# Where the side work of an attention loop stands: extra steps of VectorE, TensorE and ScalarE moved to the slots with long matmul bursts, and two small products moved from VectorE to ScalarE

## The reference

```python
x = x + tanh(g_xattn) * xattn(layernorm(x), ctx, mask, mask, Wq, bq, Wk, bk, Wv, bv)
x = x + tanh(g_ffn)   * ffn(layernorm(x), W2, scale, scale1)

# xattn: 16 heads of 32 channels
q, k, v = Wq @ t + bq, Wk @ s + bk, Wv @ s + bv
dot  = (q^T k) / sqrt(32); dot = mask * dot - (1 - mask) * 1e6
out  = (softmax(dot) * mask) @ v^T

# ffn: both inputs rounded to FP8, then one matmul
q1, q2 = (layernorm(x) * scale).astype(FP8), (W2 * scale1).astype(FP8)
return (q1 / scale) @ (q2 / scale1)
```

## Time and profile before

| | us |
|---|---|
| median of three runs | 2848.67 |
| the profiled execution's own time | 2844.43 |
| its span, first to last instruction | 2842.6 |
| TensorE busy / VectorE busy | 2643.0 / 2155.0 |
| GpSimd busy / ScalarE busy | 1726.9 / 1456.4 |

### The profile page before, as it was taken

One profiled execution on the slowest core, in us unless ns is written; L12 is line 12 of the kernel. 1 busy time (PEld: TensorE's weight loads), 2 busy tenths in 40 slices (PEclk: granted clock), 3 DMA queues, 4 the chain that ended last, 5 costly groups with the idle time before them and its releaser, 6 DMA issues. The chain is left out here.

```text
span 2842.6 us, 41049 instructions
## 1 busy us (share of the span) xinstructions
PE 2643.0 (93%) x13364; PEld 1373.5 (48%) x13425; DVE 2155.0 (76%) x3314; ACT 1456.4 (51%) x2574; POOL 1726.9 (61%) x1265
## 2 busy tenths in 40 slices
PE   5999999959999999999999999999999999999995
PEld 4888888834444444444444444444444444444441
DVE  5666666656787878778888888888878888788873
ACT  3333333315555555555555555555555555555553
POOL 2333333416676767667767667677667667667774
PEclk8999999959999999999999999999999999999998
DMA  6666666454333333333333333334434443333301
GB/s 213 244 233 222 237 246 233 178 118 84 70 78 80 81 82 77 77 77 77 77 77 78 77 77 81 85 80 87 86 79 84 86 87 82 77 77 77 78 28 38
DMA packets 208249, 306.12 MB, mean 108 GB/s; under 512 B 41240, under 2 KB 108888, under 8 KB 208064
## 3 DMA queue, kind: packets, MB, share of 16 engines
q1 hardware_dynamic: 195920, 265.80, 38.8%
q10 hardware_dynamic: 12144, 38.02, 3.8%
HBM read 200.09 MB, written 102.11 MB: 106 GB/s over the span
## 5 line engine op out<-in xcount | busy, mean ns | idle before, releaser
L965 POOL TENSOR_TENSOR pair_sum<-probs 128x512 f32<-128x512 f32 x1024 | 1359.2, 1360 | 618.5 <-ACT probs L802 618.5
L866 DVE TENSOR_REDUCE part_max<-x_bank 128x1 f32<-128x512 f32 x2048 | 1308.5, 681 | 401.3 <-PE x_bank L709 394.3
L802 ACT ACTIVATE probs<-s_bank 128x512 f32<-128x512 f32 x2048 | 1129.2, 600 | 877.1 <-PE s_bank L696 859.9
L709 PE MATMUL x_bank<-k_st,q_st 98*128 98x512 f32 x2048 | 889.5, 438 | 114.4 <-DVE part_max L866 75.1
L696 PE MATMUL s_bank<-q_st,k_st 100*128 100x512 f32 x2048 | 899.0, 441 | 10.3 <-ACT probs L802 5.2
L696 PEld LDWEIGHTS s_bank<-q_st,k_st 100*128 100x128 f32 x2048 | 390.2, 191 | 490.2 <-issue 240.8
L709 PEld LDWEIGHTS x_bank<-k_st,q_st 98*128 98x128 f32 x2048 | 394.2, 193 | 387.1 <-DVE part_max L866 275.4
L722 PE MATMUL o_bank<-probs,v_t 128*32 128x512 f32 x4096 | 552.2, 612 | 0.0
L733 PE MATMUL d_bank<-pair_sum,ones 128*32 128x512 f32 x2048 | 267.8, 595 | 0.9 <-POOL pair_sum L965 0.9
L321 POOL TENSOR_TENSOR stage_lo<-stage,stage_hi 128x512 fp32r<-128x512 f32 x128 | 187.4, 1487 | 120.3 <-ACT stage_hi L391 119.6
L391 ACT ACTIVATE stage_hi<-stage 128x512 fp32r<-128x512 f32 x128 | 79.9, 633 | 190.7 <-DVE stage L475 142.1
(11 more groups left out here) (98 smaller groups left out, 2277.5 us busy)
## 6 DMA issues: line engine op xcount, KB each, us to landing
k_st<-k_scr SPq DMA_DIRECT2D x96, 512.0 KB
q_st<-q_scr SPq DMA_DIRECT2D x192, 256.0 KB
c_raw<-in_ctx_dram ACTq DMA_DIRECT2D x32, 512.0 KB, 7.1
x_raw<-in_x_dram ACTq DMA_DIRECT2D x32, 512.0 KB, 6.1
k_scr<-stage_hi SPq DMA_DIRECT2D x64, 256.0 KB, 2.4
k_scr<-stage_lo SPq DMA_DIRECT2D x64, 256.0 KB, 2.6
v_scr<-stage SPq DMA_DIRECT2D x64, 256.0 KB, 2.7
q_scr<-stage_hi SPq DMA_DIRECT2D x64, 256.0 KB, 2.1
```

Of the source, the lines that this page charges most:

```text
L709: nc.tensor.matmul(x_bank_of("tile", k)[:, :], q_st[p][0:KX, th, h, tc * P:(tc + 1) * P], k_st[p][0:KX, h, sh * HALF:(sh + 1) * HALF], sta ...
L802: nc.scalar.activation(probs[:, c % PR, h, :], s_bank[S_BANK_OF[k]][:, :], ACT.Exp).then_inc(exp_done, 1)
L866: nc.vector.tensor_reduce(part_max[:, th, sh, at:at + 1], x_bank_of("tile", k)[:, :], AX, ALU.max).then_inc(max_done, 2)
L965: nc.gpsimd.tensor_tensor(pair_sum[:, r % 2, h], probs[:, a, h], probs[:, a + 1, h], ALU.add).then_inc(pair_done, 1)
```

## The change

All four moves concern the attention loop. Side work of VectorE is gathered behind the tiles of the slots in which TensorE has a burst (k = 3, 11, 19, 23, 35, 43, 51, 55, 59). TensorE's turns go from slots 10, 24, 54 to 27, 23, 55, and the FFN halves from 13/14 and 27/28 to 34/35 and 50/51, and within their slot they now stand ahead of the burst. ScalarE's copies follow them. `weigh` moves on GpSimd from behind the third group of pair sums to behind the fourth. SyncE's list is put in the order of the new slots. And `rss` and `nb2` are computed on ScalarE; for that `scl` has a second column with the negative scale, which costs one 128x1 instruction in the setup.

```diff
-            F_JOBS = {10: "turn_y8", 13: "ffn0", 24: "max1", 27: "ffn1", 54: "max0"}
+            F_JOBS = {23: "max1", 27: "turn_y8", 34: "ffn0", 50: "ffn1", 55: "max0"}
...
+                            if k == 27 and real(n - 2):
+                                turn_y8(n, k, n - 2)
+                            if k == 23 and real(n):
+                                turn_max(n, k, n, 1)
+                            if k == 55 and real(n + 1):
+                                turn_max(n, k, n + 1, 0)
+                            for half, at_ in ((0, 34), (1, 50)):
+                                if k in (at_, at_ + 1) and real(n - 2):
+                                    ffn(n, at_, n - 2, half, range(4 * (k - at_), 4 * (k - at_) + 4))
                             if k % 4 == 3:
                                 if k >= 7 and real(n):
                                     times_v(n, p, (k - 7) // 4)
...
+                    def scale_rstd(m):
+                        act.wait_ge(rs2_done, m + 1)
+                        nc.scalar.activation(rss[:, :], scl[:, :], ACT.Copy, scale=rs2[:, 0:1]).then_inc(norm_done, 1)
+                        act.wait_ge(norm_done, NORM_STEPS * m + 7)
+                        nc.scalar.activation(nb2[:, :], mv2[:, 0:1], ACT.Copy, scale=rss[:, 1:2]).then_inc(norm_done, 1)
...
-                            if k == 48 and real(n - 1):
+                            if k == 50 and real(n - 1):
+                                scale_rstd(n - 1)
+                            if k == 51 and real(n - 1):
                                 normalize(n - 1, 1 - p)
...
-                    NORM_AT = {36: 2, 37: 3, 39: 4, 40: 5, 44: 6, 45: 7, 53: 9, 56: 10, 60: 11}
-                    NORM_AT_2 = {0: 12, 3: 13, 6: 14}
+                    NORM_AT = {43: (2, 3), 44: (4,), 45: (5,), 59: (9, 10)}
+                    NORM_AT_2 = {3: (11,), 11: (12,), 19: (13, 14)}
...
-                            if r == 2 and real(n - 1):
+                            if r == 3 and real(n - 1):
                                 weigh(n - 1)
-                            if r == 3 and real(n - 1):
                                 add_residual(n - 1, 1 - p)
```

More of the change, by code:

```diff
@@ L239, in _ @@
                         chain(nc.vector.tensor_copy(g1[:, :], gt[:, 0:1]))
-                        chain(nc.vector.tensor_copy(scl[:, :], gl[:, 2:3]))
+                        chain(nc.vector.tensor_copy(scl[:, 0:1], gl[:, 2:3]))
+                        chain(nc.vector.tensor_scalar(scl[:, 1:2], gl[:, 2:3], -1.0, None, ALU.mult))
                         chain(nc.vector.tensor_copy(scl1[:, :], gl[:, 3:4]))
@@ L779, in period @@
                                     denominators(n - 1, 6 + k // 8)
[L780 to L788, removed]
                     run(period)
@@ L899, in norm @@
                         x1 = res[p]
-                        if step != 4:
-                            dve.wait_ge(norm_done, NORM_STEPS * m + step)
+                        dve.wait_ge(norm_done, NORM_STEPS * m + step)
                         if step in (2, 3):
@@ L933, in period @@
                             m, odd, i = maxima_at(n, k)
-                            if NORM_AT.get(k) == 4 and real(n - 1):
-                                dve.wait_ge(norm_done, NORM_STEPS * (n - 1) + 4)
                             if real(m):
                                 maximum(m, i, k)
[L938 to L942, removed]
-                                negate_max(n, 1)
-                            if k == 20 and real(n - 1):
+                            if k == 19 and real(n):
+                                negate_max(n, 1)
+                            if k == 51 and real(n + 1):
+                                negate_max(n + 1, 0)
+                            if k == 35 and real(n - 2):
+                                add_ffn(n - 2, p, 0, 34)
+                            if k == 51 and real(n - 2):
+                                add_ffn(n - 2, p, 1, 50)
+                            if k == 23 and real(n - 1):
                                 invert(n - 1, 1)
-                            if k == 51 and real(n):
+                            if k == 55 and real(n):
                                 invert(n, 0)
[L948 to L953, removed]
+                            if real(n - 1):
+                                for step in NORM_AT.get(k, ()):
+                                    norm(n - 1, 1 - p, step)
+                            if real(n - 2):
+                                for step in NORM_AT_2.get(k, ()):
+                                    norm(n - 2, p, step)
                     run(period)
@@ L1072, in period @@
                         if real(n):
+                            set_max(n, 1, p)
+                        if real(n - 1):
+                            spread_inv(n - 1, 1)
+                        if real(n):
                             load_tm(n)
                         if real(n):
-                            set_max(n, 1, p)
+                            move_den(n, 0)
                         if real(n - 2):
```

24 lines of the change are left out of this document (10 added, 14 removed).

## The result

The changed kernel is slower by 1.2%, which is clear of the noise. Its median is 2885.43 us (four runs, 2881.81 to 2886.61), beside 2850.43 us for the kernel before on the same chip (2847.47 to 2857.50). The ratio is 1.0119, with a 95% interval of 1.0103 to 1.0135. The forecast was 2789 with a range from 2736 to 2838. The profiled execution took 2884.45 us, its span is 2882.7, and TensorE's mean granted clock is 0.943 instead of 0.974.

What follows compares the result with a forecast made beforehand. TensorE bounds the kernel, losing 7.4 us per 68.4 us period to waits; next the stack binds. Stack-bound period 64.9 + clock 1.5 + overhang 0.3 = 66.7 us, 59.4 us saved in all: 2789 us, range 2736 to 2838.

Steps and rivals of the forecast that it cites:

- VectorE at the bursts: Side-work blocks in TensorE's bursts take their short durations, some 1.5 us free; 0.3 us per period charged.
- The rival in which the blocks overhang because GpSimd makes them long: GpSimd still works beside VectorE's blocks; 0.6 us more at slot 59, period 67.3 us, 2807 us; chance 0.14.
- Scale products, `weigh`: Two products on ScalarE at 0.25 us each, cost 0; `weigh` behind the fourth pair sums hidden to within 0.1 us.
- Turns and FFN halves: On TensorE, same instructions ahead of the burst, 3.4 + 1.0 + 0.6 = 5.0 us per period; nothing saved there.
- The floor: TensorE, never held, needs about 61.0 us per period, against 68.4 before.
- The overhang that was charged at slot 19: VectorE's block at slot 19 takes 1.7 us; 0.3 us per period charged for its overhang and small waits.
- The landing of the stack: Stack lands 20.7 us behind its issue, TensorE needs it at 16.8: 3.9 us wait per period; residual overlap 0 to 0.5.
- The clock: Behind slot 19's wait TensorE runs at 1.2 GHz for one stretch, losing 1.5 us per period; bounds 0 and 3.1.
- The rival of two slow stretches: Two slow-clock stretches per period cost 3.1 us: period 68.3 us, 2836 us; chance 0.10.
- Slower: Rival: three slow-clock stretches, 4.5 us, plus overhang at slot 59, 0.6: period 70.3 us, 2894 us; chance 0.12.
- The stack that doesn't bind: Rival: no wait for the stack, period 61.0 + 0.3 us, 7.1 us less per period, 2633 us; chance 0.05.

Runs made afterwards that it cites:

- e6: e5 with VectorE's six FP8 steps back at their old slots, between tiles: 2793.67 us, ratio 0.9804.
- e9: e5 with `weigh` back behind the third pair sums on GpSimd: 2648.12 us, ratio 0.9298.
- e5: Changed kernel with V and residual loads issued behind load_tm and the first half of q loaded half a period earlier: 2646.42 us, ratio 0.9288.
- e2: Changed kernel with the residual load moved from just ahead of the stack to the next period: 2841.64 us, ratio 0.9970.
- e4: Changed kernel with both the residual load and the load of V issued behind load_tm, about slot 30: 2837.15 us, ratio 0.9957.
- e3: Changed kernel with twenty filler matmuls on TensorE ahead of slot 19's wait for the stack: 2829.81 us, ratio 0.9941.
- e7: Changed kernel with the early half of q alone, V and residual loads left at their places: 2662.80 us, ratio 0.9350.

## Why the prediction was wrong

The wait for the stack and the slow clock behind it were foreseen, but both terms of slot 19 were sized too small, and the unhindered period too; since only 1.7 us per period were forecast as saved, an error of 2.9 turned the sign.

*VectorE at the bursts: right.* The short durations were taken for the blocks, and they hold (the rows answer to the earlier trace rows):

```profile
L97 DVE TENSOR_TENSOR y<-y,big x32: 1215/1216/1224, 766.8 to 2867.9; 128x1024 f32<-128x1024 f32 x32
L102 DVE TENSOR_SCALAR isnan<-y x32: 419/420/1387, 786.3 to 2870.4; 128x1024 bf16<-128x1024 bf16 x32
L103 DVE TENSOR_TENSOR y<-y,isnan x32: 691/693/1660, 786.8 to 2870.9; 128x1024 bf16<-128x1024 bf16 x32
```

The median of L97 is 1.216 us instead of 2.274, that of L102 0.420 instead of 1.246. e6 ties it to the place. The Trainium skill (GPSIMD Engine Reference, Specifications) says that GpSimd shares its SBUF interfaces with VectorE and contends with instructions that have two SBUF inputs or run in a 2-port performance mode; the durations of L97, with its two inputs, agree. The rival in which the blocks overhang because GpSimd makes them long fell.

*Scale products, `weigh`: right, nothing. Turns and FFN halves: not tested by themselves.* The products take 0.306 and 0.294 us on ScalarE for the 0.25 that was taken:

```profile
L832 ACT ACTIVATE rss<-scl,rs x32: 297/306/308, 750.0 to 2864.5; 128x2 f32<-128x2 f32 x32
L834 ACT ACTIVATE nb<-mv,rss x32: 294/294/296, 750.3 to 2864.9; 128x1 f32<-128x1 f32 x32
```

ScalarE's copy does wait 2.2 us for `weigh` in each period (the third row of the waits above), which the burst hides; e9 shows no cost.

*The floor: 0.6 short.* Unhindered, a period takes 61.94 us (e5) and not 61.0 + 0.3. Two steps hold most of it. An FFN half adds 1.91 us (31 to 35 and 47 to 51 take 4.98 instead of 3.07) where 1.72 was taken, 0.4 for the two. And the step from 59 to 63 takes 4.28 us instead of 3.92, in the kernel before as well; the prediction counted it among the unhindered ones. The overhang that was charged at slot 19 did not come: the step from 19 to 23 takes 4.39 us, and 0.47 of it is the turn of maxima that now stands ahead of the burst of slot 23. With L102 and L103 away from that burst (e6) it takes 4.36.

*The landing of the stack: the step that failed, first half.* The prediction took 20.7 us from quads 1 and 2, and 0 to 0.5 us for the residual load. In the changed kernel the tile comes 22.23 us behind the issue in the mean, right behind the landing. e2 shows that 1.0 of this is the residual load, which is issued 3.7 us ahead of the stack; in the kernel before it was issued 6.0 us ahead (1707.02 against the stack of the earlier trace rows):

```profile
1707.02 0.40 SPq L1059 DMA_DIRECT2D res<-in_x_dram  x1
```

Its new place beside the stack was seen and was priced too low. The other 0.5 was there before the change: by the semaphore events of that trace the stack of quads 3 to 30 landed 21.2 us behind its issue in the mean (20.3 to 22.4), unseen because the tile came at 22.8. The two landings that showed, of the first quads, were at the short side; that they lay 0.1 us apart was taken for a precision that they did not have.

*The clock: second half.* One fall of 3.4 us was taken as the pattern, with 1.5 us of loss. Here 22 of 28 slow stretches last 6.8 us. The longer idle time (5.4 us here, 3.1 there) is not the reason, since in e4 holes of 3.2 us in the mean bring stretches of 6.8 as well. The fall that was taken was one of the short kind: of the six that followed in the same trace four lasted 6.8 us, and in the periods in which such a stretch fell ahead of slot 19 the tile came 25.2 to 25.4 us behind the issue instead of 22.8, a price of 2.4 us. The loss beyond the wait is 0.38 (from the tile to the burst 0.72 instead of 0.34) and 1.8 (from 19 to 23 6.19 in the mean, where e5 has 4.39): 2.2 us. e3 took it away, and by its period and its later tile that is worth 2.1. The rival of two slow stretches had 3.1 for it, and the rival *Slower*, with 46 us more and a chance of 0.12, came nearest to the time by luck: its 4.5 us for the clock and its overhang did not come, and the late landing that did is not in it.

The sum with the measured terms: 22.2 + (61.9 - 16.8) + 2.2 = 69.5 us, against 69.63 measured. The three errors are 1.5 + 0.6 + 0.7 = 2.8, which takes 66.7 to 69.5. Why the stack by itself takes 20 us is known only in part: some 17 us with the DMA engines busy at about 200 GB/s, and a tail of about 3 us in which they are mostly idle (e4). What limits the rate and what makes the tail remain open.

*The stack that doesn't bind.* The rival with 2633 had a chance of 0.05, rightly as the changed kernel stands; e5 made it true and came to 2646. The gain that was looked for was there nearly in full (6.5 us per period in e5, of the 7.1 of this rival), and in the changed kernel slot 19 took it.

## What to carry to other kernels

Before an engine is freed from one wait, work out when it will come to the next transfer and compare that with the landings of the steady periods, not with the two that happened to show; here 17 us of need stood against 20 to 22 us of landing, and the gain of 5.95 us in the slots ahead of it was handed back there. A wait of TensorE that comes in every period is to be priced with the slow clock behind it (here 2.2 us on top of some 5; waits of up to 1.7 us in e7 had none), and a few filler matmuls tell what it costs. Then cure the wait by issuing part of the transfer earlier: e7, with the early half of q alone, turned a loss of 1.2% into a gain of 6.5%, and the two other moved loads made it 7.1%.

## What the runs showed of the hardware

The landing of the stack hardly depends on what runs beside it: 20.2 us with nothing of size, 22.2 with 1 MB of V and residual around it, 15.4 without a quarter of it: about in proportion to the bytes. The rate is 164 GB/s over the landing in e4, 201 GB/s while the DMA engines are all busy. DMA: Bandwidth & Descriptors of the Trainium skill, in its Bandwidth section, has 341 GB/s for a load of 1 MB issued from GpSimd; these loads are issued from SyncE and each fills 32 partitions, and the trace does not agree with that figure here.

Twenty bf16 matmuls of 128x512 in the hole (4.49 us) were enough to keep TensorE at 2.4 GHz over a hole of some 5 us: 1 slow stretch instead of 28. The holes of e4, 3.2 us in the mean, still brought 29 of them.
